# Attention and routed experts on one core: x plus bias formed in the prologue, rounded weight chunks in two buffers, the last block's x tiles loaded during the last unit

## The reference, cut to what matters

```
latents = layernorm(x)                                   # x: 2048 x 256
ln = layernorm(latents) * g + b;  cn = layernorm(ctx) * g + b    # ctx: 1601 x 192, masked
q = ln @ Wq.T;  k, v = concat(cn @ Wkv.T, ln @ Wlkv.T)   # 4 heads of 64
attn = softmax(rms(q) * qn_g * 64**-0.5 @ (rms(k) * kn_g).T, masked)
x = x + (attn @ v) @ Wo.T + bo                           # bo: the bias of the change
y = layernorm(x)
p = softmax(y @ router.T);  two best of 8 experts, weights renormalized
x = x + sum over the two: (silu(y @ gate) * (y @ up)) @ w2
```

## Time and profile before

| | before |
|---|---|
| median of three runs | 1138.31 us (1138.18 to 1139.41) |
| the profiled execution | 1141.2 us, span 1139.2 us |
| TensorE busy | 983.2 us, 86% |
| VectorE busy | 653.5 us, 57% |
| GpSimd busy | 594.1 us, 52% |
| ScalarE busy | 477.6 us, 42% |
| the chain that ended last | PE 47%, POOL 20%, issue 10%, ACT 8%, DVE 8%, DMA 5% |
| moved by DMA | 85.15 MB, mean 75 GB/s |

### The profile page before, as it was taken

One profiled execution on the slowest core, in us unless ns is written; L12 is line 12 of the kernel. 1 busy time (PEld: TensorE's weight loads), 2 busy tenths in 40 slices (PEclk: granted clock), 3 DMA queues, 4 the chain that ended last, 5 costly groups with the idle time before them and its releaser, 6 DMA issues.

```text
span 1139.2 us, 15241 instructions
## 1 busy us (share of the span) xinstructions
PE 983.2 (86%) x4556; PEld 638.2 (56%) x4557; DVE 653.5 (57%) x1311; ACT 477.6 (42%) x751; POOL 594.1 (52%) x460
## 2 busy tenths in 40 slices
PE   2799779999999899898999999999882469999994
PEld 2565445555555555555554554555442458888883
DVE  3889776666666566566566566566125624444442
ACT  1456524455445446445455545454431022233231
POOL 4000018766974864854955855846820025556552
PEclk9899879999999999999999999999975579999998
DMA  6000002112111212121112212122169093332332
GB/s 173 1 1 1 9 5 72 54 56 70 61 61 65 71 55 70 57 69 65 61 61 70 65 56 75 56 65 75 56 262 367 16 360 48 54 51 51 51 52 27
DMA packets 66240, 85.15 MB, mean 75 GB/s; under 512 B 10283, under 2 KB 62444, under 8 KB 64140
## 3 DMA queue, kind: packets, MB, share of 16 engines
q1 hardware_dynamic: 49166, 56.57, 14.6%
q0 software_dynamic: 7488, 10.23, 5.5%
q10 hardware_dynamic: 9534, 17.70, 4.3%
HBM read 49.87 MB, written 34.60 MB: 74 GB/s over the span
## 4 chain that ended last, share of the span: by engine, by line
PE 47%; POOL 20%; issue 10%; ACT 8%; DVE 8%; DMA 5%; ACTq 2%; DVEq 0%; POOLq 0%; SPq 0%
POOL acc_p L417 16%; PE bPV L1249 10%; ACT PT L644 5%; PE bS L1238 4%; PE bM L1169 4%; POOL wraw L421 4%; PE bS L1239 3%; PE bA L1116 3%; DMA x2t<-x 2%; PE bG L1328 2%; DVE mpart L862 2%; PE bH L1345 2%; PE bV L1133 2%; PE bG L1330 1%; PE bG L1329 1%
## 5 line engine op out<-in xcount | busy, mean ns | idle before, releaser
L862 DVE TENSOR_REDUCE mpart<-bM 128x1 f32<-128x464 f32 x492 | 295.6, 635 | 178.8 <-PE bM L1169 177.6
L417 POOL TENSOR_TENSOR acc_p<-acc_p,PT 128x1024 f32<-128x1024 f32 x144 | 343.8, 2387 | 33.6 <-ACT PT L644 29.3
L644 ACT ACTIVATE PT<-bS 128x1024 f32<-128x1024 f32 (+1 forms) x240 | 232.2, 993 | 64.8 <-PE bS L1239 58.4
L1249 PE MATMUL bPV<-PT,V 128*64 128x512 f32 x928 | 233.1, 610 | 0.0
L1238 PE MATMUL bS<-Q,S 128*128 128x512 f32 x464 | 190.0, 409 | 3.8 <-ACT PT L644 1.5
L1169 PE MATMUL bM<-S,Q 128*128 128x464 f32 x492 | 175.1, 414 | 12.1 <-DVE mpart L862 7.0
L1239 PE MATMUL bS<-Q,S 128*128 128x512 f32 x464 | 183.9, 396 | 0.0
L417 POOL TENSOR_TENSOR acc_p<-PT 128x1024 f32<-128x1024 f32 x16 | 41.6, 2601 | 255.9 <-ACT PT L644 255.9
L615 ACT CAST whi<-wraw 128x256 fp32r<-128x256 f32 x96 | 38.9, 405 | 248.3 <-POOL wraw L421 245.1
L1169 PEld LDWEIGHTS bM<-S,Q 128*128 128x128 f32 x492 | 85.0, 191 | 97.4 <-DVE mpart L862 67.6
L1238 PEld LDWEIGHTS bS<-Q,S 128*128 128x128 f32 x464 | 88.2, 190 | 56.6 <-issue 22.7
(11 more groups left out here) (221 smaller groups left out, 1461.9 us busy)
## 6 DMA issues: line engine op xcount, KB each, us to landing
wraw<-w SPq DMA_DIRECT2D x96, 128.0 KB, 2.3
wsp_d<-whi SPq DMA_DIRECT2D x96, 128.0 KB, 2.2
wsp_d<-wraw SPq DMA_DIRECT2D x96, 128.0 KB, 1.7
W<-wsp_d ACTq DMA_DIRECT2D x8, 1536.0 KB, 18.9
W<-wsp_d SPq DMA_DIRECT2D x8, 1536.0 KB, 11.7
V<-x SPq DMA_DIRECT2D x1, 2048.0 KB, 12.8
x<-x ACTq DMA_DIRECT2D x12, 128.0 KB, 2.0
out<-x ACTq DMA_DIRECT2D x12, 128.0 KB, 1.9
```

Source lines behind the costliest of these rows:

```text
L417: pool.tensor_tensor(acc_p[:], one, PT[:, q % NPT, :, :], ALU.add).then_inc(sem("z_p"), 1)
L644: act.activation(PT[:, p % NPT, 0:n, :], bS[(w.h + p) % 2][:, 0:n, :], ACT.Exp).then_inc(sem("exp"), 1)
L862: dve.tensor_reduce(mpart[:, i, g:g + 1], banks[k % len(banks)][:, 0:PIECE], AX, ALU.max)\
L1249: last = pe.matmul(bPV[b * D:(b + 1) * D, 0, :], V[:, c, h * D:(h + 1) * D], PT[:, p % NPT, b, :], start=c < 2, stop=c >= NK - 2, skip_gro ...
```

## The change

It has three parts.

*x plus bias in the prologue.* After its mask column for tile t, from t = 3 on, GpSimd adds the bias to tile t - 3 of x, still in `V`, into one of two buffers `xbs`; the last four adds follow the last mask column. SyncE stores each sum to a new DRAM tensor `xb_d`. ScalarE's copy that overwrites a tile of `V` waits for that tile's add, and ScalarE waits for all stores before the first unit. The adds in the units and after them are gone, and what loaded x loads `xb_d`. The mask columns no longer run in a loop.

*Two buffers for the rounded chunk.* `whi` has two halves, with a semaphore for the stores of each. The rounding copy of chunk n waits for the store of chunk n - 2 and for the remainder of chunk n - 2. `wraw` has two halves as before.

*The last block's x.* `x2t` lies where `Q1` and `Q2` of the even heads lie. ScalarE issues the four loads in the last unit (an odd head) after exponential 2. VectorE waits for the loads itself, and before it writes the table `G`, which shares that memory, it waits for the stores of the four tiles.

```diff
+            xb = xb_d.rearrange("(t p) d -> t p d", p=P)
+            for t in range(NT):
+                sp.wait_ge(sem("xb"), t + 1)
+                sp.dma_start(xb[t, :, :], xbs[:, t % 2, :]).then_inc(sem(f"xb_st{t % 2}"), 16)
...
-            sp.wait_ge(sem("pv"), NP * UNITS)
-            for i in range(QB):
-                sp.dma_start(x2t[:, i, :], xt[NF + i, :, :]).then_inc(sem(f"xin_t{i}"), 16)
...
+            def x_bias(t):
+                if t >= 2:
+                    pool.wait_ge(sem(f"xb_st{t % 2}"), 16 * (t // 2))
+                pool.tensor_tensor(xbs[:, t % 2, :], V[:, NC + t, :], bob[:], ALU.add).then_inc(sem("xb"), 1)
+
+            pool.wait_ge(sem("c_bo"), 16)
+            for t in range(NC + 2):
+                k_mask(Step(None, t))
+                if t == 3:
+                    pool.wait_ge(sem("x_in"), 16)
+                if t >= 3:
+                    x_bias(t - 3)
+            for t in range(NC - 1, NT):
+                x_bias(t)
...
-                    if n == XB_AT and w.fin:
-                        pool.wait_ge(sem("xin"), 16 * w.tile + 16)
-                        pool.tensor_tensor(x2[:], x2[:], bob[:], ALU.add).then_inc(sem("xb"), 1)
...
-            for i in range(QB):
-                pool.wait_ge(sem(f"xin_t{i}"), 16)
-                pool.tensor_tensor(x2t[:, i, :], x2t[:, i, :], bob[:], ALU.add).then_inc(sem("xb"), 1)
...
+                    if b == 'l':
+                        act.wait_ge(sem("xb"), t.back(NC).v + 1)
...
-                after(act, sem("wst_h"), 16 * n)
-                after(act, sem("wsplit"), n)
-                act.copy(whi[:], wraw[:, n % 2, :]).then_inc(sem("whi"), 1)
+                after(act, sem(f"wst_h{n % 2}"), 16 * (n // 2))
+                if n > 1:
+                    act.wait_ge(sem("wsplit"), n - 1)
+                act.copy(whi[:, n % 2, :], wraw[:, n % 2, :]).then_inc(sem("whi"), 1)
...
+            def x_load_last():
+                act.wait_ge(sem("s_mm"), NP * (UNITS - 1))
+                for i in range(QB):
+                    act.dma_start(x2t[:, i, :], xt[NT - QB + i, :, :]).then_inc(sem(f"xin_t{i}"), 16)
...
+            dve.wait_ge(sem("ox_t"), 16 * QB)
             link(dve.tensor_tensor(G[:], flat.unsqueeze(2).to_broadcast([P, R, NBLK + 1]),
```

More of the change, by code:

```diff
@@ L110, in build @@
           router_t, w13, w2, out):
+    xb_d = nc.dram_tensor("xb_d", [TOK, DIM], F32, kind="Internal").ap()
     xln_d = nc.dram_tensor("xln_d", [TOK, DIM], F32, kind="Internal").ap()
@@ L181, in build @@
         rt = sb("rt", [P, 2, E], at=big)
-        bob = sb("bob", [P, DIM], at=big)
         lg = sb("lg", [P, NT, E], at=big)
@@ L191, in build @@
         qn = sb("qn", [P, 2, DIM], at=t0)
+        bob = sb("bob", [P, DIM], at=t0)
+        xbs = sb("xbs", [P, 2, DIM], at=t0)
         m_u8 = sb("m_u8", [P, NC], U8, at=t0)
@@ L206, in build @@
         t1 = ExitStack()
-        Q1 = sb("Q1", [P, 2, QW], F32R, at=t1)
-        Q2 = sb("Q2", [P, 2, QW], F32R, at=t1)
+        tq = ExitStack()
+        QQ = sb("QQ", [P, 2, 2, QW], F32R, at=tq)
+        Q1, Q2 = QQ[:, :, 0, :], QQ[:, :, 1, :]
+        tq.close()
+        x2t = sb("x2t", [P, 2 * QB, DIM], at=t1)
         PT = sb("PT", [P, NPT, 2, QW], at=t1)
@@ L211, in build @@
         wraw = sb("wraw", [P, 2, WC], at=t1)
-        whi = sb("whi", [P, WC], F32R, at=t1)
+        whi = sb("whi", [P, 2, WC], F32R, at=t1)
         t1.close()
@@ L216, in build @@
         t2 = ExitStack()
-        x2t = sb("x2t", [P, QB, DIM], at=t2)
         x3t = sb("x3t", [P, QB, DIM], at=t2)
@@ L329, in _ @@
                 sp.wait_ge(sem("whi"), n + 1)
-                sp.dma_start(wsp_d[e, 0, :, c:c + WC], whi[:].bitcast(F32)).then_inc(sem("wst_h"), 16)
+                sp.dma_start(wsp_d[e, 0, :, c:c + WC], whi[:, n % 2, :].bitcast(F32)).then_inc(sem(f"wst_h{n % 2}"), 16)
                 sp.wait_ge(sem("wsplit"), n + 1)
@@ L335, in _ @@
                     load(n + 2)
-            xt = x.rearrange("(t p) d -> t p d", p=P)
             ot = out[0:TOK, :].rearrange("(t p) d -> t p d", p=P)
@@ L420, in w_lo @@
                 pool.wait_ge(sem("whi"), n + 1)
-                pool.tensor_tensor(wraw[:, n % 2, :].bitcast(F32R), wraw[:, n % 2, :], whi[:].bitcast(F32),
+                pool.tensor_tensor(wraw[:, n % 2, :].bitcast(F32R), wraw[:, n % 2, :], whi[:, n % 2, :].bitcast(F32),
                                    ALU.subtract).then_inc(sem("wsplit"), 1)
@@ L648, in unit @@
                         x_load(w.tile)
+                    if p == 2 and w.last:
+                        x_load_last()
                     if p in SPLIT_AT:
@@ L661, in unit @@
                     c_row(v, w.next_h % 2)
+            for k in range(2):
+                act.wait_ge(sem(f"xb_st{k}"), 16 * NT // 2)
             q_hi(0, 0, 0)
@@ L666, in _ @@
             run_units(unit)
-            act.wait_ge(sem("wst_h"), 16 * E * NCH)
             for k in range(2):
+                act.wait_ge(sem(f"wst_h{k}"), 16 * E * NCH // 2)
                 act.wait_ge(sem(f"wst{k}"), 16 * E * NCH // 2)
@@ L904, in stats2 @@
             def stats2(t, x_, y, st, mv):
-                dve.wait_ge(sem("xb"), t + 1)
                 dve.wait_ge(sem("y_mm"), t + 1)
@@ L925, in unit @@
                     if p == Y_AT and w.fin:
+                        dve.wait_ge(sem("xin"), 16 * t + 16)
                         stats2(t, x2[:], bT[:, 0, 0:DIM], st2[:], mv2[:])
@@ L963, in _ @@
                 if i < QB:
+                    dve.wait_ge(sem(f"xin_t{i}"), 16)
                     stats2(NF + i, x2t[:, i, :], bFY[i][:, 0, 0:DIM], st2t[:, i, :], mv2t[:, i, :])
@@ L1398 @@
 OUT_AT, HEADS_AT, Y_AT, SD_AT, X3_AT, X3T_AT, LG_AT = 5, 7, 8, 9, 10, 11, 12
-XB_AT = 2
 SPLIT_AT, LO_AT = (1, 3, 5, 7, 9, 11), (1, 3, 5, 7, 9, 9)
```

6 lines of the change are left out of this document (1 added, 5 removed).

## The result

| | before | after |
|---|---|---|
| median of the runs beside each other | 1138.86 us (1138.18 to 1139.88) | 1100.42 us (1099.95 to 1101.6) |
| the profiled execution | 1141.2 us, span 1139.2 | 1101.6 us, span 1099.9 |
| TensorE busy | 983.2 us, 86% | 976.9 us, 89% |
| VectorE busy | 653.5 us | 661.1 us |
| GpSimd busy | 594.1 us | 594.1 us |

Both medians are of four runs. The ratio is 0.9663, with a 95% interval of 0.9647 to 0.968. The forecast was 1101.9, between 1091 and 1114. The spans differ by 39.3 us. Both profiles are cut at the first unit's first sum, the start of each unit (its first sum on GpSimd), the end of the last output product, the read of the logits, and the end.

The account below looks back on a forecast made before the run. TensorE was taken to bound the units, its waits hanging on ScalarE behind rounding copies. Terms -23.9 - 3.0 - 12.1 + 2.6 = -36.4 us gave 1104.8 profiled, 1101.9 for the median, range 1091 to 1114.

Parts of the forecast that it names:

- The later units: Eleven later units: ScalarE's copies come sooner, so TensorE waits less; -23.9 us, between 8 and 26.6 us gained.
- the routing wait: Later units: TensorE's wait before the routing product, for ScalarE's `x3T`, 11.0 us in all or 1.0 each, would be covered.
- The wait for the turn: Five later units: TensorE's wait before the turn of x3, for VectorE's norm; 0.6 of 1.4 us each would stay.
- Rival (b): Later units: ScalarE's wait only changes its name, store and load taking 5.5 us, not 4.4; 1121 us, chance 0.09.
- I take it that it waits too: VectorE's norm, with one tensor in SBUF, is locked out beside a GpSimd sum; bounds nothing to 2.4 us.
- rival (a): VectorE's one-input operations are not locked out by GpSimd, so prologue, units and last unit do better; 1095.4 us, chance 0.24.
- an add follows each mask copy: Prologue: GpSimd's adds lock out VectorE's `xn`, 0.25 us late in some ten meetings; +2.6 us.
- I take 3.0 us: Last unit: TensorE's 4.79 us wait for the turn of x3 shrinks; 3.0 us gained, between 0 and 5.
- After the last unit: Last output product to logits: x is already loaded, so VectorE waits only for the projection; -12.1 us.
- the same stores took 5.1 us in the median: After the last unit: the stores of x2 land before table G is written, so that wait costs nothing, 10 us to spare.
- rival (c): After the last unit: the stores of x2 land late and the routing loses 2 to 7 us; about 1106 us, chance 0.07.
- Rival (d): TensorE, fed with hardly a gap, is granted a lower clock; 1173 us at a clock of 0.90, chance 0.03.

Follow-up runs that it names:

- the copies tied: Changed kernel with each rounding copy waiting for the residual and store of the chunk just before, as with a single buffer: 1119.2 us, ratio 0.9823.
- the doubled additions: Changed kernel with each prologue addition of x and bias made twice on GpSimd, the first into a scratch tile: 1105.01 us, ratio 0.9706.
- the root first: Changed kernel with ScalarE's root for the norm of x ahead of its rounding copy in the twelve later units: 1098.53 us, ratio 0.9637.

## Why the prediction was right, point by point

**The later units.** Forecast -23.9, measured -23.6. The terms 0.9 and 1.15 us that the sum has for the routing wait stand in no row ahead of it; the trace of the kernel before has them, 0.85 to 0.90 us in the units with a projection and 1.15 in the others. The two parts were shown apart, 17.8 for the second buffer and 6.4 for the bias add; the forecast had the bias add at 8, so the buffer at 16. The wait for the turn that would stay was put at 5 x 0.6 = 3.0 us and is 3.2, but it is spread otherwise: 0.4 us in five units, and 1.15 in one with a projection, where the root was late. Rival (b) is out: the residual's round of store and load became what releases ScalarE, but at 102.5 us in place of 245, and with the copies tied the units went back to 43.

**The lock.** "I take it that it waits too" was right, so rival (a) is out: 412 ns became 1079, and `xn` 0.91 beside a doubled addition. With the copies tied, where the ninth sum stands as in the changed kernel but the norm comes only at its end, it took 413 ns again. The measured time lies near the forecast and not at (a)'s 1095.4, though that alone would prove little, since errors of 2 to 3 us cancel in it (below). The Trainium skill, "SBUF — State Buffer", section "Who interferes with whom", has the lock for any VectorE operation in a two-port mode; the trace agrees, with up to 2.50 us for a norm that takes 0.41 alone.

**The prologue.** The failed step is "an add follows each mask copy, from 34.25 to 35.0 ... and `xn` starts at 34.75": +2.6 us, measured -0.1. I had let the addition start at the end of the mask copy as the earlier trace rows show it and beyond. It starts 0.14 us after the copy's start, ends at 34.73, and `xn` begins at 34.70. The mechanism was right and its time was 0.25 us off, as the doubled additions showed with their +3.4 to +4.5 us; only one `xn` was held up, 0.73 us where two additions ran into it.

**The first unit.** It was taken as unchanged, and 1.6 of the 39.3 us fell there. The changed kernel and its variants gave the short length ten times and the long one three times, so it may be chance. Of the kernel before there is one profile, with the long one: that the change has no part in it is not shown. Without it the two profiles differ by 37.7 us.

**The last unit.** The failed step is "I take 3.0 us"; it gained 0.65. The copy ahead of the root starts 2.3 us sooner after the unit's first sum, as was forecast ("some 2 us"), and waits for its chunk now; the norm starts 2.3 us sooner too, and the lock takes 1.3 of that back (1.69 us for 0.41). So the turn comes only 1.0 us sooner, and 0.35 of it was lost behind it. The timeline (start us, us, instruction, idle before):

```profile
796.94 0.40 ACT L629 CAST whi<-wraw 128x256 fp32r<-128x256 f32 x1 [3.28 <-DMA wraw<-w]
...
799.28 1.69 DVE L939 TENSOR_SCALAR x<-x,mv,rs 128x256 f32<-128x256 f32 x1
...
801.02 0.69 PE L1227 MATMUL bT<-ident,x 128*128 128x128 f32 x2 [5.21 <-DVE x L939]
801.64 3.68 PE L1274 MATMUL bPV<-PT,V 128*64 128x512 f32 x8
```

and in the kernel before:

```profile
828.03 3.68 PE L1249 MATMUL bPV<-PT,V 128*64 128x512 f32 x8
```

The wait was 4.79 and is 5.21, since TensorE too comes to it sooner. After it the eight output products take 3.68 us, as they did before; at the full clock eight take 1.94. The clock fell in both kernels, 0.91 in the mean of the unit, so this is no loss of the change but a gain that it did not bring. With the root first the turn came at 798.69 and took 0.44 us instead of 0.69, the unit's clock was 0.95, and the last unit was 1.9 to 2.3 us shorter: the root behind the copy was the cause for the larger part of what was missing, and that copy's chunk is what was late next. I had asked that question for the later units and not for this one, where no piece of next maxima fills TensorE's time.

**After the last unit.** Forecast -12.1, measured -13.6. The first addition was put 9.5 us behind the last product and came 9.8 behind it. From the end of the projections to the logits 6.4 us were forecast and 4.9 came: the turns and routing products, 5.4 us of TensorE at the lower clock, took 4.0 from 828 on, at a mean clock of 0.79. Why the clock was up there is not shown. The eight issues of weights ahead of the output's copy, 4.16 us, were not read as a cost; they are there in both kernels, and moving them away gave 2.2 us up to the first addition and 3.0 up to the logits.

**The stores.** The failed step is "the same stores took 5.1 us in the median ... with 10 us to spare". They took 15.5 us in the median and 16.8 at most; the last issue, at 830.56, landed by 847.4, and G was written at 848.03. So the mechanism of rival (c) was there, and only its price was nil, by luck. Before, the first of these stores left 27 us after the first issue of weights (837.34 to 864.0), with most of that transfer done; now it leaves 13 us after it (811.35 to 824.13), in the middle. The Trainium skill, "DMA: Bandwidth & Descriptors", section "Queues, rings and completion order", has the engines take turns between queues by packets; the prediction set it aside for a row taken at another moment. With the weights' loads moved behind the stores the landing took 2.4 us: the trace agrees that the two queues held each other up, and does not show the turns themselves.

**The clock.** Rival (d) is out: 1.00 inside the later units, 0.948 in the whole against 0.942.

**The sum.** It was forecast at 36.4 us and the profiles differ by 39.3. It came this near in part by luck: the prologue was put 2.7 us too dear, the stretch after the last unit 1.5 too low and the first unit's 1.6 not at all, against 2.35 us too much for the last unit.

## What to carry to other kernels

Ask of each engine's order what an operation will meet at its new time, to a tenth of a microsecond: here a 0.7 us addition on an engine that idles a third of the time cost 0.6 us in each unit, most of it through the lock, and the same addition cost nothing in the prologue. A landing time read from a row holds for the traffic at that moment; where a change moves transfers, take it from a moment with the traffic they will meet. Look at what stands in front of the engine that ends a stretch: issues of transfers that are not urgent, and a small root behind a copy that waits for a load, were each worth 2 to 3 us.

## What was not expected of the hardware

- A VectorE norm of 128x256 with one tensor in SBUF takes 0.41 us alone and up to 2.50 us beside a GpSimd sum of 128x1024 of 2.4 us. What counts is what it meets: started earlier it became longer in the last unit (1.69 to 2.50 us) and shorter in the later ones (0.61 in the median with the norm ahead of the reductions).
- In 14 profiles TensorE's clock in the first unit went with a small difference of idle time and with the moment at which it had risen: waits of 1.16 to 1.92 us left it at the full level, waits of 2.03 to 2.14 us, each after an earlier rise, were followed by the lower one, and the unit was 1.6 us longer.
- Stores of 128 KB landed 15.5 us in the median after their issue while loads of 1536 KB were under way in another queue, and 2.4 us after it without them.
